# One VectorE instruction in place of sixteen: scaling 16 heads by dt in a Mamba-2 layer on 8 cores

## What is computed

```
hs = hs.reshape(b, L, H, P)
X = (hs * dt[..., None]).reshape(b, nchunk, CH, H, P)
Y_diag = jnp.einsum('bclsh,bcshp->bclhp', M, X)
decay_states = jnp.exp(A_cs[..., -1:] - A_cs)
B_decay = Bc * decay_states.transpose(0, 2, 3, 1)[..., None]
states = jnp.einsum('bclhn,bclhp->bchpn', B_decay, X)
```

## Time and profile before

| | us |
|---|---|
| runs of the kernel, median of 3 (lowest to highest) | 10897.81 (10896.49 to 11099.11) |
| the profiled execution | 10990.76 |
| its span on core 0, the slowest | 10989.2 |
| spans of cores 1 to 7 | 10881.1 to 10964.0 |
| busy on core 0: TensorE | 5169.2 (47%) |
| busy on core 0: VectorE | 3415.4 (31%), 7083 instructions |
| busy on core 0: ScalarE, GpSimd | 451.7 (4%), 200.3 (2%) |

### The profile page before, as it was taken

The page is one execution under the profiler, slowest core; times in us unless marked ns, Lnnn a source line. Parts: engine busy times, 40 slices in busy tenths (PEclk is TensorE's granted clock), DMA queues, the critical chain, the costliest instruction groups (busy, mean ns, idle before and its releaser), DMA issues.

```text
span 10989.2 us, 79833 instructions; the slowest of 8 cores (10881.1 to 10989.2 us)
## 1 busy us (share of the span) xinstructions
PE 5169.2 (47%) x25402; PEld 2498.8 (23%) x25402; DVE 3415.4 (31%) x7083; ACT 451.7 (4%) x467; POOL 200.3 (2%) x344
## 2 busy tenths in 40 slices
PE   2268888666666667899211101101110110487585
PEld 0035555333333323433111000000000000133232
DVE  5620000232232233300455343443443444200101
ACT  1100000000000000000000100000000000000000
POOL 0000000000000000000000000000000000000000
PEclk9998888877777778977555555555555555688787
DMA  1123333221122122333111212112112111455555
GB/s 61 75 54 62 59 62 63 50 39 39 39 41 39 37 41 45 60 67 67 46 60 52 99 39 55 44 27 59 44 23 63 45 43 39 95 109 113 155 111 130
DMA packets 329934, 673.29 MB, mean 61 GB/s; under 512 B 231477, under 2 KB 258741, under 8 KB 281269
## 3 DMA queue, kind: packets, MB, share of 16 engines
q0 software_dynamic: 45376, 389.24, 19.4%
q1 hardware_dynamic: 265846, 260.60, 7.3%
q10 hardware_dynamic: 18304, 18.36, 0.5%
HBM read 878.30 MB, written 112.74 MB: 90 GB/s over the span
## 4 chain that ended last, share of the span: by engine, by line
PE 45%; DVE 28%; DMA 11%; issue 10%; ACT 3%; DVEq 2%; another core or an unknown queue 1%; SPq 0%; ACTq 0%; POOLq 0%
PE pP L399 23%; PE pQ0f L1176 5%; PE pQ1f L1176 5%; DMA fill<-scr_acs 5%; PE pQ0d L582 3%; PE pQ1d L582 3%; DVE xdec_a L724 2%; DVE xdec L1020 2%; DVE tmpX L1109 1%; DVE fill L982 1%; DVEq L127 1%; ACT lmat L1003 1%; DVE hbc_sb L442 1%; DVE acc L370 1%; DVE acc L366 1%
## 5 line engine op out<-in xcount | busy, mean ns | idle before, releaser
L399 PE MATMUL pP<-xn_T,wbuf 128*128 128x429 bf16 (+4 forms) x13920 | 2567.0, 349 | 24.6 <-DMA wbuf<-w_in_s 13.8
L399 PEld LDWEIGHTS pP<-xn_T,wbuf 128*128 128x128 bf16 x13920 | 1425.6, 103 | 1139.7 <-issue 202.4
L1030 PE MATMUL pYde<-xdec,lmat 128*128 128x64 bf16 x1024 | 64.7, 239 | 1585.0 <-DVE xdec L1020 1585.0
L1176 PE MATMUL pQ0f<-nrm_sb,wbc 128*128 128x512 bf16 x2048 | 508.5, 415 | 199.1 <-DMA nrm_sb<-scr_n 172.7
L442 DVE COPY hbc_sb<-pP 128x429 f32<-128x429 f32 (+2 forms) x240 | 143.0, 596 | 1406.1 <-PE pP L399 1389.6
L1176 PE MATMUL pQ1f<-nrm_sb,wbc 128*128 128x512 bf16 x2048 | 507.2, 414 | 28.2 <-DVE rb L1197 28.2
L582 PE MATMUL pQ0d<-xn_T,wbuf 128*128 128x512 bf16 x1024 | 457.9, 447 | 75.6 <-DVE bse_a L591 56.6
L461 PE MATMUL pT0b<-ident_sb,accs 128*128 128x128 bf16 x320 | 84.8, 265 | 823.2 <-ACT accs L454 738.1
L582 PE MATMUL pQ1d<-xn_T,wbuf 128*128 128x512 bf16 x1024 | 458.4, 448 | 0.0
L425 DVE COPY tbuf<-pT0b 128x128 bf16<-128x128 bf16 x256 | 57.5, 224 | 1237.2 <-PE pT1b L421 1184.9
L1030 PEld LDWEIGHTS pYde<-xdec,lmat 128*128 128x128 bf16 x1024 | 56.3, 127 | 1636.3 <-issue 1636.3
(11 more groups left out here) (171 smaller groups left out, 4539.7 us busy)
## 6 DMA issues: line engine op xcount, KB each, us to landing
wbuf<-w_in_s POOLq DMA_DIRECT2D x145, 1024.0 KB, 8.0
wbc<-w_out_s POOLq DMA_DIRECT2D x64, 2048.0 KB, 15.2
fill<-scr_acs POOLq DMA_DIRECT2D x64, 1024.0 KB, 7.8
wbuf<-w_ffn_s POOLq DMA_DIRECT2D x32, 1024.0 KB, 8.3
xt_sb<-x SPq DMA_DIRECT2D x9, 2048.0 KB
xt_sb<-x_oth SPq DMA_DIRECT2D x9, 2048.0 KB
scr_g<-tbuf SPq DMA_DIRECT2D x64, 256.0 KB
scr_hs<-tbuf SPq DMA_DIRECT2D x64, 256.0 KB
```

Of the source, the lines that this page charges most:

```text
L399: run(PE, cPE, lambda e, ps=ps, wb=wb, off=off, ln=ln, dc=dc: e.matmul(ps[:, 0:ln], wb[:, dc * 128:(dc + 1) * 128], xn_T[:, dc * XNW + off ...
L1030: run(PE, cPE, lambda e, i=i: e.matmul(pYd[:, i * 64:(i + 1) * 64], lmat[:, i * 128:(i + 1) * 128], xdec[:, i * 64:(i + 1) * 64], start=Tr ...
L1176: run(PE, cPE, lambda e, wb=wb, cc=cc, pq=pq: e.matmul(pq[:, :], wb[:, cc * 128:(cc + 1) * 128], nrm_sb[:, cc * 512:(cc + 1) * 512], start ...
```

## The change

At each of the three places the 16 instructions of 128 x 64, each with a column of the float32 table as its per-partition factor (tensor_scalar), become one instruction of 128 x 1024 (tensor_tensor). It reads the 16 interleaved pieces of X by one access pattern, and as its second tensor the 16 columns of the table, each repeated 64 times by a stride of zero. The factors and the output keep their types. Waits before and after are the same.

```
-                for i in range(16):
-                    h = 8 * i + g
-                    run(VE, cV, lambda e, h=h, i=i: e.tensor_scalar(
-                        xdec[:, i * 64:(i + 1) * 64], tmpX[:, h * 64:(h + 1) * 64],
-                        dtT[:, h:h + 1], None, ALU.mult))
+                run(VE, cV, lambda e, g=g: e.tensor_tensor(
+                    xdec[:, :].rearrange("l (i u p) -> l i u p", u=1, p=64),
+                    tmpX[:, :].rearrange("l (i g p) -> l i g p", g=8, p=64)[
+                        :, :, g:g + 1, :],
+                    dtT[:, :].rearrange("l (i g) -> l i g", g=8)[
+                        :, :, g:g + 1].rearrange("l i (g u) -> l i g u", u=1
+                        ).broadcast_to((128, 16, 1, 64)),
+                    ALU.mult))
                 xd_v = cV.n
```

More of the change, by code:

```diff
@@ L658, in build_nc @@
                     VE.wait(cPE, st_pe)
-                for i in range(16):
-                    h = 8 * i + g
-                    run(VE, cV, lambda e, h=h, i=i: e.tensor_scalar(
-                        xdec_a2[:, i * 64:(i + 1) * 64], tmpX_a2[:, h * 64:(h + 1) * 64],
-                        dtdecT[:, h:h + 1], None, ALU.mult))
+                run(VE, cV, lambda e, g=g: e.tensor_tensor(
+                    xdec_a2[:, :].rearrange("l (i u p) -> l i u p", u=1, p=64),
+                    tmpX_a2[:, :].rearrange("l (i g p) -> l i g p", g=8, p=64)[
+                        :, :, g:g + 1, :],
+                    dtdecT[:, :].rearrange("l (i g) -> l i g", g=8)[
+                        :, :, g:g + 1].rearrange("l i (g u) -> l i g u", u=1
+                        ).broadcast_to((128, 16, 1, 64)),
+                    ALU.mult))
                 xd_v = cV.n
```

## The result

The changed kernel took 10455.2 us as the median of nine runs (10281.84 to 10598.27). The kernel before, run again beside it, took 11083.49 us as the median of ten (10896.49 to 11589.07). The ratio of the two kernels is 0.944, with a 95% interval from 0.9419 to 0.9461; the forecast was 10280.5 / 10897.8 = 0.943. In many executions of either kernel the cores of one die, or of both, have a lower TensorE clock in some stage and end 90 us to several hundred us later; so both medians stand high, and what follows compares the lowest times (10896.5 us before, 10281.8 us after) or the median span of a die that kept its clock.

What follows compares the result with a forecast made beforehand. It took a chain passing between engines, none full, to bound the changed stages: 809.1 us removed less 191.8 added is 617.3 us, off the median 10897.8 giving 10280.5 us, range 10190 to 10395.

Steps and rivals of the forecast that it cites:

- The chain: State loops and main loop: engines wait for one another once per group, so all the sixteen take is on the path.
- What is removed and added: Three changed places, 144 groups: 809.1 us of the sixteen go, 191.8 us of single instructions come, 617.3 us saved.
- The cost from L1068: The new instruction takes 1225 ns, like a main-loop multiply sharing its operands, types and size.
- the gap of 0.107 us: Idle time ahead of each new instruction, taken as that ahead of the first of the sixteen.
- the 470 us: Smaller gain of the whole change by the skill page's estimate of 181 ns per old instruction, against 241 ns traced.
- What could be late next: State-stage stores and copies, main-loop loads and DMA, TensorE's clock: none becomes a new limit; all costed at nothing.
- The double rate: Rival: the new instruction takes 691 ns, bringing 77 us more, 10204 us; chance 0.04.
- The state stage met no limit: Rival: denser stores make the copy wait for its buffer, giving back up to 275.3 us, 10555.8 us; chance 0.04.
- restart at the pieces: Rival: the new instruction's access pattern restarts at each of 16 pieces, up to 8650 ns, 11350 us; chance 0.03.
- The time: Whole kernel: 617.3 us off the runs' median of 10897.8 us gives 10280.5 us, 5.7% less.
- a stage outside the three that changes its length: Sign of being wrong: any stage besides the two state loops and the main loop changes its length.

Runs made afterwards that it cites:

- Each part alone: Single instruction in the state stage's two loops only, or the main loop only, against the kernel before: 10550.2 us; 10616.5 to 10622.5 us.
- the second's: The changed kernel run once more, nothing altered, with the kernel before beside it: median 10488.6 us over 11 runs.

## Why the prediction was right and wrong

**The chain.** Right. The sixteen stood on the path with all their time. Each part alone, the whole, and the instruction given twice fall within 9 us of the sums.

**What is removed and added.** Right: 809.1 us were to give way to 191.8, and 192.1 stand there now. The cost from L1068 was right to a nanosecond, and the gap of 0.107 us ahead of it too (6.7 / 64 = 0.105). The gain by the lowest times is 614.7 us, the forecast was 617.3, and the 470 us that the prediction set against it did not come. What the removed 809.1 us were made of was not in the prediction: it had 241 ns as each instruction's own time, and without the waits one starts every 146 ns.

**What could be late next.** Right in the main: no copy into sgrp waits for a store, and TensorE's clock in these stages stays at 0.50. VectorE's wait for the exponential in the main loop moved by a few microseconds only: on core 0 from 753.0 to 761.0 us, on core 4 from 756.8 to 753.4 us, so this is no cost of the change.

**The rivals.** The double rate did not come, and the two kernels with another second tensor show what it would take. The state stage met no limit, and no restart at the pieces is seen: 692 ns for sixteen such pieces at the double rate leaves none.

**The time.** This is the step that failed: the level from which the gain was taken off, and the room for the difference between runs. I took the median of three runs, 10897.8 us, as the kernel's level. Over ten runs its median is 11083.5 us, 186 us higher, and the changed kernel's is 10455.2 us, 175 us above my 10280.5. The ratio came out all the same because both medians stand high by about as much. Above the forecast the range had little more than the profiled execution's 93 us, with "some run-to-run difference" added without a row behind it. Two things that I had in front of me said more. One of the three runs had taken 11099.11 us, 201 us above the others. And die 0 ended 75 us later at a lower clock in one execution; I placed that difference before the stages of the change, rightly, and took the level of die 1 for the kernel's, without asking in how many executions a die falls behind, and by how much. It does not belong to the die: in the changed kernel's profile the other die is the later one. What differs is the clock in a stage full of products. In the kernel before it was the base product of the feed-forward layer. On core 0, with a granted clock of 0.76 to 0.84 between 4620 and 5200 us, and then on core 4, with 0.99:

```profile
L582 PE MATMUL pQ1d<-xn_T,wbuf 128*128 128x512 bf16 x1024 | 458.4, 448 | 0.0
```

```profile
L582 PE MATMUL pQ1d<-xn_T,wbuf 128*128 128x512 bf16 x1024 | 393.2, 384 | 4.3 <-DVE bse_a L591 2.1
```

In the changed kernel both cores have 383 ns there, and it is the output projection that differs. On core 0, with a granted clock of 0.80 to 0.88 in stretches of it, and on core 4, with 0.68 to 0.74:

```profile
L1185 PE MATMUL pQ1f<-nrm_sb,wbc 128*128 128x512 bf16 x2048 | 506.9, 414 | 27.9 <-DVE rb L1206 27.9
```

```profile
L1185 PE MATMUL pQ1f<-nrm_sb,wbc 128*128 128x512 bf16 x2005 | 596.0, 471 | 34.6 <-DVE rb L1206 31.8
```

With its twin on the other buffer (594.4 and 506.0 us) this is 1190 us of products on core 4 against 1013 us on core 0, 177 of the 184 us between their spans. Neither stage was touched. The prediction named a stage outside the three that changes its length as a sign of being wrong, and this is that sign. A range for the time as it is measured had to reach at least those 201 us above 10280.5, to 10481 us, and it would have held the first series' median, 10455.2 us, and missed the second's, 10488.6 us, by 8 us. Why a die gets the lower clock in one execution and not in the next stays open; no run here tells.

## What to carry to other kernels

A run of small instructions on one engine, each waiting for the one before, is worth looking for wherever another engine waits for the last of them: find it by the count, the idle time before the line and the gap in the timeline, and price its replacement by a row with the same operand types and the same repeat. Before making such work cheaper, ask whether it has to stand between the wait and its reader at all; here the same sixteen instructions a few lines earlier gained more in the main loop than their replacement did. And forecast a ratio from the chain and a time from the spread of the runs: the highest of three runs is part of the evidence.

## What the runs showed of the hardware

- Small VectorE instructions overlap when no wait stands between them: 128 x 64 in bf16 with a per-partition factor lasts 235 to 241 ns, but one can start every 146 ns; with a wait for the one before, one started every 348 ns. The Trainium skill (VectorE: DVE Perf Modes, section Side-by-side) gives about 158 cycles of setup and fill for each, 181 ns with its elements by an estimate; the trace has more for one alone and less for one of a row.
- A second tensor repeated by a step of zero keeps a tensor_tensor in bf16 at 1225 ns for 1024 elements; with adjacent elements, in pieces of 64 with gaps, it takes 692 ns.
- The lower TensorE clock came in one stage of an execution, the base product in one profile and the output projection in others, and lengthened products of 128 x 512 from 384 to 448 ns and from 414 to 471 ns. It need not take a die as a whole: in the profile of the sixteen without their waits it took cores 0 and 1 in the input projection (371 ns for products of 128 x 343, 334 ns on core 2) and cores 2 and 3 in the output projection (462 to 464 ns, 414 to 415 ns on cores 0 and 1).
